# Attention layer: maxima search mixed with the second head group, transposed reciprocals, and q/k stacks filled by DMA alone

## The reference

```python
qkv = jnp.einsum('bcij,oc->boij', x, w_qkv) + b_qkv[None, :, None, None]
q = qkv[:, :C] * scale;  k = qkv[:, C:2 * C];  v = qkv[:, 2 * C:]
# for each pixel: scores against the 49 pixels of its 7x7 window (zero padded),
# softmax over the 49, weighted sum of v, then
# out = einsum(out, w_proj) + b_proj
```

## Time and profile before

| what | us |
|---|---|
| median of three runs | 4197.12 |
| the profiled execution's own time | 4211.27 |
| its span | 4209.5 |
| convolution, stretch 0 to 368 | 368 |
| attention, stretch 368 to 1717 | 1349 |
| scans, stretch 1717 to the end | 2492 |
| TensorE busy in the span | 3749.5 (89%) |
| VectorE busy | 3086.7 (73%) |
| ScalarE busy | 2041.0 (48%) |
| GpSimd busy | 2309.8 (55%) |

### The profile page before, as it was taken

How to read it: one execution, slowest core, us unless ns; L and a number is a source line. 1 busy time by engine, 2 the same in 40 slices (tenths; PEclk the granted TensorE clock), 3 DMA queues, 4 the chain that set the end, 5 groups by cost and what they waited for, 6 DMA issues and landing times.

```text
span 4209.5 us, 120863 instructions
## 1 busy us (share of the span) xinstructions
PE 3749.5 (89%) x49136; PEld 2316.1 (55%) x49136; DVE 3086.7 (73%) x3557; ACT 2041.0 (48%) x2707; POOL 2309.8 (55%) x877
## 2 busy tenths in 40 slices
PE   4995799899899898499999999999999999999998
PEld 4994666666666666245444444554555454444444
DVE  6564667667657665378887888888888788888887
ACT  2332344444444443265555555555665555555553
POOL 1111121121121120188888888888888888888887
PEclk9997899999999999699999999999999999999999
DMA  9724133233233232436555555556565555555643
GB/s 100 90 45 111 55 102 107 71 101 108 71 96 113 71 93 55 115 89 137 131 113 121 126 119 124 117 124 145 113 143 113 131 131 119 122 119 124 146 104 92
DMA packets 346994, 453.11 MB, mean 108 GB/s; under 512 B 64649, under 2 KB 218893, under 8 KB 346433
## 3 DMA queue, kind: packets, MB, share of 16 engines
q1 hardware_dynamic: 345104, 444.06, 47.0%
q10 hardware_dynamic: 1362, 1.39, 0.1%
HBM read 301.69 MB, written 94.37 MB: 94 GB/s over the span
## 4 chain that ended last, share of the span: by engine, by line
PE 30%; SPq 11%; issue 6%; DMA 5%; POOL 4%; DVE 3%; ACT 1%; DVEq 0%; POOLq 0%; ACTq 0%
PE ssm_u_ps L861 11%; PE ssm_y_ps L874 10%; SPq L766 6%; PE ssm_scratch L891 4%; DMA ssm_b_diag<-ssm_b_blocks 4%; POOL ssm_h L1256 3%; DVE ssm_h L1173 2%; PE ssm_u_ps L936 2%; SPq L747 2%; PE ssm_scratch L901 1%; SPq L736 1%; SPq L717 1%; PE ssm_scratch L916 1%; DMA ssm_b_blocks<-ssm_b_t 1%; SPq L723 1%
## 5 line engine op out<-in xcount | busy, mean ns | idle before, releaser
L1256 POOL TENSOR_TENSOR ssm_h<-ssm_h,ssm_c_rep 128x2048 f32<-128x2048 f32 x384 | 1752.9, 4570 | 231.6 <-DVE ssm_h L1173 203.2
L1173 DVE TENSOR_TENSOR_SCAN ssm_h<-ssm_decay,ssm_h,ssm_u_ps 128x512 f32<-128x512 f32 x768 | 935.8, 1260 | 211.6 <-PE ssm_u_ps L861 211.6
L861 PEld LDWEIGHTS ssm_u_ps<-ssm_b_diag,ssm_dx_t 64*64 64x64 f32 x24576 | 754.2, 136 | 550.1 <-issue 538.0
L861 PE MATMUL ssm_u_ps<-ssm_b_diag,ssm_dx_t 64*64 64x128 f32 x24576 | 936.6, 292 | 128.1 <-DMA ssm_b_diag<-ssm_b_blocks 78.9
L1173 DVE TENSOR_TENSOR_SCAN ssm_h<-ssm_decay,ssm_u_ps 128x512 f32<-128x512 f32 x768 | 892.1, 1203 | 131.0 <-PE ssm_u_ps L861 103.8
L1010 ACT ACTIVATE ssm_decay<-ssm_delta_rep,ssm_a_neg 128x1024 f32<-128x1024 f32 x768 | 849.6, 1144 | 226.7 <-DVE ssm_h L1173 212.0
L874 PE MATMUL ssm_y_ps<-ssm_h,ssm_state_sum 128*64 128x512 f32 x3072 | 773.6, 626 | 6.1 <-POOL ssm_h L1256 6.1
L1783 ACT ACTIVATE l_probs<-l_work 128x532 f32<-128x532 f32 (+1 forms) x384 | 217.3, 566 | 558.5 <-PE l_work L1637 551.8
L874 PEld LDWEIGHTS ssm_y_ps<-ssm_h,ssm_state_sum 128*64 128x64 f32 x3072 | 191.8, 140 | 319.7 <-issue 309.0
L1952 DVE RECIPROCAL l_den<-l_den 96x1024 f32<-96x1024 f32 x32 | 209.6, 6548 | 194.2 <-ACT l_den L1796 194.2
L2035 POOL TENSOR_TENSOR l_rstd<-l_var_eps,l_minus_half 96x2 f32<-96x2 f32 x16 | 11.1, 693 | 585.7 <-DVE l_var_eps L1872 585.7
(11 more groups left out here) (162 smaller groups left out, 5340.9 us busy)
## 6 DMA issues: line engine op xcount, KB each, us to landing
ssm_c_rep<-ssm_c_by_state SPq DMA_DIRECT2D x256, 512.0 KB, 7.0
ssm_delta_rep<-ssm_delta SPq DMA_DIRECT2D x384, 128.0 KB, 3.6
l_qk_parts<-l_qk SPq DMA_DIRECT2D x48, 768.0 KB, 4.7
ssm_b_diag<-ssm_b_blocks SPq DMA_DIRECT2D x1024, 32.0 KB, 3.2
ssm_x<-x_after_l SPq DMA_DIRECT2D x32, 768.0 KB, 6.1
ssm_x_res<-x_after_l SPq DMA_DIRECT2D x192, 128.0 KB, 4.4
l_x<-x SPq DMA_DIRECT2D x64, 192.0 KB, 9.0
x_after_l<-l_x SPq DMA_DIRECT2D x64, 192.0 KB, 4.1
```

The source lines that it names most:

```text
L861: made = nc.tensor.matmul(u_ps[64 * par:64 * par + 64, ring("u", w), r, at:at + 128], dx_t[rows, db, 2 * win + k, 64 * g:64 * g + 64], of_ ...
L1173: nc.vector.tensor_tensor_scan(h[:, s % S_RING, npi, t], decay[:, 2 * (s % 2) + npi, t], u, start, ALU.mult, ALU.add).then_inc(scanned, 1)
L1256: nc.gpsimd.tensor_tensor(view, view, c_rep[:, 2 * q:2 * q + 2, :], ALU.mult).then_inc(c_applied, 1)
```

## The change

1. The 24 fills that search maxima for batch n + 1 are no longer done alone ahead of `pass_b(n, 1)`: eight come first, and the others are put between the score and value steps of the second head group (`MIXED`). The units of `work` are renumbered.
2. `divide` becomes six steps: transpose the denominators in 32x32 blocks, take one column of each block (the 32 rows of a head hold the same number), reciprocal of [96, 32] in place of [96, 1024], two transposes back, two products. For group 0 the six steps are put behind the maximum searches 10 to 15.
3. `copy_stacks` goes; `move_parts` loads each part to all of its places from DRAM (6, 4 and 2 places for the parts 0, 1 and 2: 24 DMAs in place of 12).
4. `to_row_layout`, `take_rows` and `move_rows` for batch n move from the end of main(n - 1) into main(n): on TensorE behind the q and k projection, on ScalarE behind `take_qk`, on SyncE behind the loads of part 0 and ahead of the parts 1 and 2.
5. `norm` comes ahead of the maxima search, VectorE's `norm_finish` too; `normalise` is cut in two (after exponentials 3 and 7); `padding_terms` comes after the last exponential.

```diff
+FIRST_SCORES = 8
+MIXED = [("a", i) for i in range(FIRST_SCORES)]
+for _i in range(UNIT_PAIRS):
+    _done = sum(kind == "a" for kind, _ in MIXED)
+    MIXED += [("b", _i)] + [("a", _done + k) for k in range(min(1 + _i % 2, 2 * UNIT_PAIRS - _done))]
+MIXED += [("a", i) for i in range(sum(kind == "a" for kind, _ in MIXED), 2 * UNIT_PAIRS)]
+PART_LANDED = (192, 128, 64)
+DIVIDE_STEPS = 6
+DIVIDE_AFTER = list(range(10, 10 + DIVIDE_STEPS))
...
+        den_t = sb("den_t", [CHUNK, L])
+        den_once = sb("den_once", [CHUNK, HEAD])
...
-                            (qk1, high_made, 3, ((0, q_a, q), (0, k_a, k))),
-                            (qk2, mid_made, 1, ((64, q_a, q), (32, k_a, k))),
+                            (qk1, high_made, 3, ((0, q_a, q), (0, k_a, k), (32, q_a, q), (64, k_a, k), (0, q_b, q), (32, k_b, k))),
+                            (qk2, mid_made, 1, ((64, q_a, q), (32, k_a, k), (96, q_a, q), (96, k_a, k))),
                             (qk3, low_made, 3, ((32, q_b, q), (0, k_b, k))))):
...
                 def main(n):        # SyncE
                     if has(n, 2):
                         sp.wait_ge(xn_made, n.count(1, 2))
                         load(Batch(n.it + 1, n.s))
                     if has(n, 1):
-                        move_parts(n)
+                        move_parts(n, (0,))
+                    if not n.first:
+                        move_rows(n)
+                    if has(n, 1):
+                        move_parts(n, (1, 2))
                     if not n.first:
                         store(n)
                         load_residual(n)
-                    if has(n, 1):
-                        move_rows(n)
...
+                def await_stacks(n):
...
+                    for part in range(3):
+                        pe.wait_ge(part_loaded[part], m.count(PART_LANDED[part], PART_LANDED[part]))
...
+                def pass_a_and_b(n):
+                    await_stacks(n)
+                    for kind, i in MIXED:
+                        if kind == "a":
+                            scores_a(n, i)
+                        else:
+                            if i == 0:
+                                start_group(n, 1)
+                            scores_b(n, 1, i)
+                            if i:
+                                values(n, 1, i - 1)
+                    values(n, 1, UNIT_PAIRS - 1)
+                    end_group()
...
                 def main(n):        # TensorE
                     if has(n, 1):
-                        project(n)
+                        project_qk(n)
+                    if not n.first:
+                        to_row_layout(n)
+                    if has(n, 1):
+                        project_v(n)
                     if not n.first:
                         project_out(n)
                     pass_b(n, 0)
-                    if has(n, 1):
-                        pass_a(n)
                     if has(n, 2):
                         norm(n)
-                    pass_b(n, 1)
                     if has(n, 1):
-                        to_row_layout(n)
+                        pass_a_and_b(n)
+                    else:
+                        pass_b(n, 1)
...
                 def main(n):        # ScalarE
                     if has(n, 1):
                         take_qk(n)
+                    if not n.first:
+                        take_rows(n)
+                    if has(n, 1):
                         middle_part(n)
...
                         exps(n, 1, i)
-                        if i == 3 and has(n, 1):
-                            padding_terms(n)
-                        if i == 7 and has(n, 2):
-                            normalise(Batch(n.it + 1, n.s))
+                        if i in (3, 7) and has(n, 2):
+                            normalise(Batch(n.it + 1, n.s), i // 4)
+                    if has(n, 1):
+                        padding_terms(n)
                     keep_acc(n, 1)
-                    if has(n, 1):
-                        take_rows(n)
...
+                def divide_step(n, g, step):
+                    k = n.count(8, 4 * g)
+                    cols = slice(step % 2 * HALF, step % 2 * HALF + HALF)
+                    if step == 0:
+                        dve.wait_ge(acc_kept, n.count(2, g + 1))
+                        nc.vector.transpose(den_t[:, :], den[:, :]).then_inc(den_inverted, 1)
+                    elif step == 1:
+                        dve.wait_ge(den_inverted, k + 1)
+                        nc.vector.reciprocal(den_once[:, :], den_t[:, :].rearrange("p (b j) -> p b j", j=HEAD)[:, :, 0]
+                                             ).then_inc(den_inverted, 1)
+                    elif step < 4:
...
+                        b = slice(step % 2 * 16, step % 2 * 16 + 16)
+                        nc.vector.transpose(den[:, cols].rearrange("p (b j) -> p b j", j=HEAD),
+                                            den_once[:, b, None].to_broadcast([CHUNK, 16, HEAD])).then_inc(den_inverted, 1)
+                    else:
+                        dve.wait_ge(den_inverted, k + step - 1)
+                        nc.vector.tensor_tensor(att[:, g, cols], att[:, g, cols], den[:, cols], ALU.mult).then_inc(att_made, 1)
...
                 def main(n):        # VectorE
...
                         take_v(n)
+                    if has(n, 2):
+                        norm_stats(Batch(n.it + 1, n.s))
                     if not n.first:
                         residual(n)
-                    if has(n, 1):
-                        copy_stacks(n, 0)
-                    if has(n, 2):
-                        norm_stats(Batch(n.it + 1, n.s))
-                    if has(n, 1):
-                        copy_stacks(n, 1)
-                        maxima(n)
                     if has(n, 2):
                         norm_finish(norm_use(n), Batch(n.it + 1, n.s))
-                    divide(n, 0)
                     if has(n, 1):
+                        maxima(n)
                         split_padding(n)
+                    else:
+                        divide(n, 0)
```

More of the change, by code:

```diff
@@ L1646, in pass_a, with scores_a, scores_b @@
                         pe.wait_ge(masks_made, 1 if n is None else 2)
-                    pe.wait_ge(stacks_copied, m.count(2, 2))
-                    pe.wait_ge(part_loaded[2], m.count(64, 64))
-                    for i in range(2 * UNIT_PAIRS):
-                        scores(a_use(n, i), m, i // UNIT_PAIRS, i % UNIT_PAIRS, q_a, q_b, k_a, k_b, 112)
+                    for part in range(3):
+                        pe.wait_ge(part_loaded[part], m.count(PART_LANDED[part], PART_LANDED[part]))
+                def scores_a(n, i):
+                    scores(a_use(n, i), after(n), i // UNIT_PAIRS, i % UNIT_PAIRS, q_a, q_b, k_a, k_b, 112)
+                def scores_b(n, g, i):
+                    scores(b_use(n, g, i), n, g, i, k_a, k_b, q_a, q_b, 114)
                 def values(n, g, i):
@@ L1720, in prologue @@
                     norm("start")
-                    project(None)
-                    pass_a(None)
+                    project_qk(None)
+                    project_v(None)
+                    await_stacks(None)
+                    for i in range(2 * UNIT_PAIRS):
+                        scores_a(None, i)
                     norm(None)
-                    to_row_layout(None)
+                    to_row_layout(ZERO)
                 def main(n):
                     if has(n, 1):
-                        project(n)
+                        project_qk(n)
[3 more added lines that the diff above has]
+                        project_v(n)
                     if not n.first:
@@ L1745, in _, with normalise @@
             def _(act):
-                def normalise(m):
-                    act.wait_ge(norm_step, m.count(7, 7))
-                    if not m.first:
-                        f = project_use(None if is_static(m, 1) else before(before(m)), 6)
-                        await_fill(act, f)
-                    for c in range(2):
-                        last = nc.scalar.activation(image(xn[:, c, :]), x[:, c, :].rearrange("p (y s x) -> p s y x", s=2, x=TILE_W), ACT.Identity,
-                                                    scale=rstd[:, c:c + 1], bias=shift[:, c:c + 1])
-                    last.then_inc(xn_made, 1)
+                def normalise(m, c):
+                    if c == 0:
+                        act.wait_ge(norm_step, m.count(7, 7))
+                        if not m.first:
+                            f = project_use(None if is_static(m, 1) else before(before(m)), 6)
+                            await_fill(act, f)
+                    done = nc.scalar.activation(image(xn[:, c, :]), x[:, c, :].rearrange("p (y s x) -> p s y x", s=2, x=TILE_W), ACT.Identity,
+                                                scale=rstd[:, c:c + 1], bias=shift[:, c:c + 1])
+                    if c:
+                        done.then_inc(xn_made, 1)
                 def take_qk(n):
```

(15 more changed lines are left out.)

86 lines of the change are left out of this document (46 added, 40 removed).

## The result

| | before | after |
|---|---|---|
| device time, median, in the shared runs | 4202.34 (4 runs, 4193.46 to 4213.19) | 4278.86 (4 runs, 4272.35 to 4284.59) |
| span of the profiled execution | 4209.5 | 4282.8 |
| attention | 1347.9 | 1432.8 |
| scans | 2485.0 | 2474.0 |
| VectorE busy | 3086.7 | 2816.1 |

The account below looks back on a forecast made before the run. TensorE, almost without a gap, bounds attention. Plain batches 8 x 5.2 and jump batches 5 x 6.9 give 76; batch 14 +6, prologue and batch 0 +6, last divides -7.6: 4197 + 80 = 4277 us, range 4170 to 4330.

Parts of the forecast that it names:

- The rows' chain: From T0 (ScalarE begins copying out the second head group) through part 0's loads until maxima rows land: T0 + 31.3.
- TensorE's readiness: TensorE, after v and output projection, is ready for `pass_b` at T0 + 25.6 and waits 5.7 us for the rows.
- The clock's fall in `pass_b`: After the wait for rows, TensorE's lower clock adds 2.3 us to each `pass_b` of group 0; bounds 0 and 3.
- The mix: Maxima searches among group 1's steps: group 0's end to T0 takes 32.6 us, gain about 3, bounds 0 and 6.
- the stack wait: Part 2's loads land by T0 + 49, group 0 ends at T0 + 49.9: a tie, no wait but nothing to spare.
- The divide: VectorE's reciprocal and product fall from 7.8 to 4.0 us, hidden except at the last two divides: 7.6 less, once.
- The sum: Plain batch +5.2, with the jump back +6.9, batch 14 +6, prologue and batch 0 +6, last divides -7.6: +80 us.
- The port rule: Partitions 0 to 63 and 64 to 127 each reach half the DMA ports; would save 1.8 us a batch; not adopted.
- The first: Rival, faster: part 0's loads run at a store's rate, the chain hides and the mix pays; middle 4165; chance 0.18.
- the second: Rival, same time: rows at T0 + 28.5, 2.9 us of wait without the clock's fall; 4205; chance 0.15.
- Hand-overs that stall the mix: Rival, slower still: VectorE's divide steps between searches cost 4 us a batch; 4330; chance 0.17 shared with no mix effect.
- VectorE's pace in the search: Rival: VectorE's searches pace the stretch, so mixing has no effect; called unlikely; chance 0.17 shared with stalls on top.

Follow-up runs that it names:

- The filler ahead of v: Five matmuls with overwritten results put between the maxima rows' transposes and v, in the version with VectorE's copies: 4190.32 us, 0.992 of the kernel before.
- VectorE's copies: Kernel after, with two places a part loaded by DMA and VectorE copying the others again: 4195.22 us, 0.9965 of the kernel before.
- v begun earlier, two kernels: Version with VectorE's copies, rows' transposes moved behind v: 4185.84 us, 0.9922; the same with `norm` early: 4166.1 us, 0.9882.
- `norm` early: Version with VectorE's copies and rows' transposes behind v, with `norm` moved ahead of `pass_b` of group 0: 4166.1 us, 0.9882 of the kernel before.

## Why the prediction was right, and where it was off

**The rows' chain.** Predicted: first load T0 + 15.8, part 0 in by 27.4, row loads issued 28.4, rows there 31.3. Measured in the batch shown: 15.4, row loads issued 28.5, `pass_b` at 30.8; over the plain batches 30.6 to 31.4. From the first row load's issue to `pass_b` it was 2.3. The prediction's terms for it, 0.6 of issuing and 2.5 of latency, make 3.1 (its own sum took 2.9), so this term, for which no row stood, was some 0.7 too high. The rate was 223 GB/s against the 219 taken from the earlier trace rows. That the chain is the cause of the wait is shown twice: without the extra places the loss is gone, and with rows ahead of them it moves to the stacks.

**TensorE's readiness.** Predicted T0 + 25.6 and a wait of 5.7 in every batch. That held in two of the 14 batches (25.1 and 5.96 in the one shown). In the others the 2.17 us stand ahead of v, which the prediction had in its times but not in its clock, made v 7.0 long (three) or 8.4 to 8.7 (nine), and the wait 2.2 to 4.6. In the kernel after this cost nothing, since the rows set the end: the row loads landed no earlier for it. The clock's fall in `pass_b`, predicted at 2.3 in all batches, cost 1.9 in the batch shown second (18.46 against 16.59), 1.4 in the one shown first (17.97) and 2.0 to 2.5 in the three where v took 7.0; the longest waits were not followed by the largest losses. Some 0.3 of the 2.3 was no clock at all: the 18.7 it rests on is counted to ScalarE's copy, the 16.3 to TensorE's last matmul. The readiness step was wrong in its mechanism and hidden in the sum. The filler ahead of v shows the cause.

**The mix.** Predicted 32.6 from group 0's end to T0. In the kernel after it was 32.7 to 34.7; with VectorE's copies it was 32.7 to 33.8 in ten of 13 batches and 36.0 in the three whose clock was 0.74 over the first 9 us of it. So the loss of round trips is as estimated, but in the kernel after some of it was taken back by the stack wait (1.71 in the batch shown; called a tie in the prediction) and by the clock behind it (0.77 from 1266.15 on). The step was mis-sized by up to 2 in a batch. Over the plain batches the stretch went from 35.8 to 33.5 in the mean, a gain of 2.3 where 3.3 was in the sum. (The prediction counts from TensorE's last matmul; by that mark each of these lengths is 0.3 more.)

**The divide.** Predicted 4.0 each and -7.6 once; measured 4.1 where GpSimd doesn't meet it and 5.6 where it does, and -3.8 and -3.5.

**The sum.** Plain 82.5 predicted, 82.7 measured; before 77.3 taken, 77.5 measured: +5.2 both. That the plain batch came out to the tenth is luck: `pass_b` begins 5.9 later (6.2 predicted), is 1.6 longer (2.3) and the mixed stretch is 2.3 shorter (3.3), and the three errors cancel. With the jump 88.2 predicted, 87.2 measured: +5.7 for +6.9. Batch 14 +9.1 for +6. The first T0 came 12.0 later than before, predicted +6 (the same stretch came 4.2 later in the kernel with the divide alone and 4.4 earlier in the one with VectorE's copies, so half of the excess or more may be chance). Together 8 x 5.2 + 5 x 5.7 + 9.1 + 12.0 - 7.3 = 84, which the attention's +84.9 confirms, for +80. Jump too high by 6, batch 14 and prologue too low by 9: they nearly cancelled. For the whole kernel 4277 was forecast and 4278.9 measured. That is closer than the working deserves: it took 4197 as the time before and added 80, while the shared runs had 4202.3 before and 76.5 more after; and the scans alone, unchanged, differ by 11 between the two profiled executions.

**The port rule.** I went by the trace and not by the rule, rightly for this kernel: with five places low and one high the rate stayed at 223. But the reason given, that one low and one high place together moved no more than two low ones, was too weak to rule the ports out: those loads were issued one place after the other, and with three and three places, issued in turn, 268 were moved. Whether the places or the order did it is open.

**The rivals.** The first (loads at the rate of a store) fell with 223 GB/s. The wait came with the clock's fall in every batch, so the second did not come about either. Hand-overs that stall the mix cost far less than 4 a batch. VectorE's pace in the search did not set that of the stretch, though TensorE stood for it at times: 30.5 us in the main part of the attention, before 24.8.

**Still open.** Why the same 2.17 us stand brings v to 5.3, 7.0 or 8.6 us, and why the clock of the mix falls to 0.74 behind `norm_finish` in some batches and not in others. Whether the ports or the order of issue made part 0's loads faster. That short stands lower the clock is shown; which of them do is not.

## What to carry to other kernels

Work taken off an engine with slack (in this kernel 10.5 us of copies a batch on VectorE) was worth nothing, and if it is turned into transfers it lands in the queue of whoever has none: write out the DMA queue's own timeline from the last store that it depends on, and put small urgent transfers in it by their due time. A step moved close to its use loses the cover that hid its latency; moving it back by one stage only helps if the next stage has slack for what it pushes. Short waits of TensorE have a second price in its clock: look at the granted clock behind each of them before calling it cheap.

## What the runs showed of the hardware that I had not expected

- The scans, with the same code throughout, took 2470.9 to 2500.4 us in ten profiled executions. One execution of a whole kernel can thus hide or fake 15 us of attention; the stage's own time can't.
- A stand of 2.17 us before v was followed by a clock of 1.00, 0.76 or 0.61 in otherwise equal batches, one of 1.09 inside v (v begun earlier, two kernels) in all 28 by 1.00. Yet with `norm` early, stands of 0.7 to 0.9 ahead of `pass_b` were followed by a clock of 0.72 over 6 us in all eight plain batches, and by 1.00 in four of the five with the jump (0.54 in the fifth).
- Part 0's transfer at a DMA share of 1.05 and 1.06 moved 223 or 268 GB/s, with the places five and one or three and three on the two sides, and the issue one after the other or in turn.
- A VectorE product of two [96, 512] float32 inputs took 0.65 us alone and 2.15 where a GpSimd subtraction of 2.12 us had begun 0.52 before it: it ended 0.55 after GpSimd had. In the kernel before, where the two began together at 1012.54, VectorE's product took its 1.22 and GpSimd's operation 3.20 in place of 2.12.
- A float32 matmul of 96x512 took 0.43 us in each of two passes (4.29 for five).
